# Attention and a patch convolution on one core: scored key tiles and kept score blocks in alternation over the whole chunk

## What is computed

```python
q = einsum('qc,bcn->bqn', Wq, xf); k = einsum('qc,bcn->bqn', Wk, xf)     # 32 rows each
v = einsum('vc,bcn->bvn', Wv, xf)                                        # 256 rows
attn = softmax(einsum('bqn,bqm->bnm', q, k) / sqrt(32), axis=-1)         # 4096 x 4096 per image
out = einsum('bvm,bnm->bvn', v, attn)
y = gamma[0] * einsum('oc,bchw->bohw', Wo, out) + x
# layer 1, per 8x8 patch p of y
low = mean of 2x2 of p;  high = p - up2(low)
low = prelu(bn(mag_w @ low + mag_b));  hs = [high, roll(high, 1, rows)]
out = up2(low) + prelu(bn(phase_w @ hs + phase_b))[:256]
```

## Time and profile before

| | before |
|---|---|
| median of 3 runs | 2342.92 us (2342.83 to 2344.77) |
| the profiled execution | 2340.45 us |
| its span, first to last instruction | 2338.5 us |
| mean granted TensorE clock | 0.984 |
| TensorE busy (matmul) | 2205.9 us, 94% of the span |
| VectorE, ScalarE, GpSimd busy | 76%, 61%, 29% |

### The profile page before, as it was taken

How to read it: one execution, slowest core, us unless ns; L and a number is a source line. 1 busy time by engine, 2 the same in 40 slices (tenths; PEclk the granted TensorE clock), 3 DMA queues, 4 the chain that set the end, 5 groups by cost and what they waited for, 6 DMA issues and landing times.

```text
span 2338.5 us, 48099 instructions
## 1 busy us (share of the span) xinstructions
PE 2205.9 (94%) x16373; PEld 1764.1 (75%) x16373; DVE 1782.4 (76%) x3388; ACT 1431.6 (61%) x2547; POOL 677.7 (29%) x891
## 2 busy tenths in 40 slices
PE   5799999999989999999998999999999999999997
PEld 4577777777767777777777777777777777777776
DVE  6777877777867788877786877777877777778764
ACT  3457666657656666666656666566665656666663
POOL 3232332232322323322232321323322232233321
PEclk8799999999999999999999999999999999999998
DMA  4254444454554444444474443443445444344443
GB/s 159 59 115 94 99 109 102 84 117 99 135 131 85 110 107 92 109 108 97 93 168 102 99 99 72 104 96 91 103 111 133 75 89 93 77 82 88 84 86 64
DMA packets 596617, 235.02 MB, mean 101 GB/s; under 512 B 547072, under 2 KB 548352, under 8 KB 596576
## 3 DMA queue, kind: packets, MB, share of 16 engines
q1 hardware_dynamic: 596576, 234.51, 45.5%
HBM read 67.67 MB, written 32.53 MB: 43 GB/s over the span
## 4 chain that ended last, share of the span: by engine, by line
PE 64%; DVE 15%; issue 10%; DMA 5%; ACT 3%; POOL 1%; SPq 1%; DVEq 0%; ACTq 0%; POOLq 0%
PE M L482 13%; PE M L519 7%; PE O L631 7%; PE O L633 6%; PE O L632 6%; PE O L644 6%; PE O L646 6%; PE O L645 6%; DVE pq L1052 5%; DMA pt<-pq 4%; PE S L590 4%; DVE saved L947 4%; DVE pmax L943 2%; DVE pl L1047 2%; PE M L500 1%
## 5 line engine op out<-in xcount | busy, mean ns | idle before, releaser
L758 ACT ACTIVATE ph<-S 128x512 f16<-128x512 f32 x512 | 307.6, 601 | 525.5 <-PE S L590 524.8
L644 PE MATMUL O<-uh,pt 128*128 128x257 f16 x2048 | 568.2, 277 | 16.9 <-DMA pt<-pq 16.7
L631 PE MATMUL O<-uh,ph 128*128 128x257 f16 x2048 | 570.3, 278 | 4.5 <-DVE pl L1047 4.1
L633 PE MATMUL O<-uh,pl 128*128 128x257 f16 x2048 | 563.2, 275 | 0.0
L632 PE MATMUL O<-ul,ph 128*128 128x256 f16 x2048 | 561.8, 274 | 0.0
L646 PE MATMUL O<-uh,pt 128*128 128x257 f16 x2048 | 559.0, 273 | 0.0
L645 PE MATMUL O<-ul,pt 128*128 128x256 f16 x2048 | 555.7, 271 | 0.0
L947 DVE TENSOR_SCALAR_CACHE_REDUCE saved<-M 128x512 f32<-128x512 f32 x512 | 344.0, 687 | 257.0 <-PE M L519 253.0
L1047 DVE TENSOR_TENSOR pl<-p,ph 128x512 f16<-128x512 f32 x512 | 402.6, 787 | 60.5 <-ACT p L761 59.1
L519 PE MATMUL M<-kst,qst 96*128 (+1 forms) x1024 | 424.0, 442 | 20.9 <-DVE saved L947 16.2
L1052 DVE TENSOR_TENSOR pq<-saved,pq 128x512 f16<-128x512 f32 x512 | 387.6, 757 | 19.2 <-ACT saved L770 19.1
(11 more groups left out here) (161 smaller groups left out, 2907.4 us busy)
## 6 DMA issues: line engine op xcount, KB each, us to landing
xr<-in_x SPq DMA_DIRECT2D x53, 512.0 KB, 3.8
out_y<-z SPq DMA_DIRECT2D x33, 512.0 KB, 3.0
xb<-in_x SPq DMA_DIRECT2D x25, 512.0 KB, 3.7
pt<-pq SPq DMA_TRANSPOSE x512, 3.1
qraw<-q_scratch SPq DMA_DIRECT2D x99, 64.0 KB, 2.0
uh_scratch<-uh_next SPq DMA_DIRECT2D x24, 257.0 KB, 3.2
uh<-uh_scratch SPq DMA_DIRECT2D x24, 257.0 KB, 3.2
ul_scratch<-ul_next SPq DMA_DIRECT2D x24, 256.0 KB, 3.1
```

The lines of the kernel that those rows point to most:

```text
L631: nc.tensor.matmul(O[j][:, 0:UW], ph[:, i % 4, q], uh[:, i, :], start=(i == 0), stop=False)
L633: ins = nc.tensor.matmul(O[j][:, 0:UW], pl[:, i % 4, q], uh[:, i, :], start=False, stop=False)
L644: nc.tensor.matmul(O[j][:, 0:UW], pt[:, k % RING, i, :], uh[:, t, :], start=False, stop=False)
```

## The change

It has three parts.

1. `UNITS` alternates from the first step: d0, k0, d1, k1, to d15, k15. Block k is weighed in step 2k + 1; its exponentials are in step 2k - 4 and its low part in step 2k - 2 (the last one a step earlier). For blocks 0 and 1, and for the low part of block 0, that is before the chunk's first step: they are made at the very start of the chunk.
2. The values in SBUF are waited for by groups of four tiles, each with a semaphore, instead of one for each half; the loads at the end of an image move to the places where their group has been used. O0 to O2 are complete with d15, so they are copied out after it (`d_weighed`), O3 after k15.
3. ScalarE waits for the next image's scale ahead of the first eviction of values, not ahead of the chunk. VectorE starts the reduction before the image (`bound_x`) and makes the scale after step 0's normalising; its first chunk of an image is written out apart from the loop for that.

In the diff, the first `copy_out` and the first `turn` are ScalarE's, the last `turn` is VectorE's.

```diff
-RISE = 6
-UNITS = [("d", i) for i in range(RISE)]
...
+UNITS = [unit for i in range(ND) for unit in (("d", i), ("k", i))]
+EXP_AT = [2 * k - 4 for k in range(NK)]
+LOW_AT = [min(2 * k - 2, MT - 5) for k in range(NK)]
...
             def weigh_tile(g, i):
-                if i == 0:
-                    pe.wait_ge(u_direct_loaded, 128 * (g // NCH) + 16)
+                if i % SUB == 0:
+                    pe.wait_ge(u_loaded[i // SUB], 32 * (g // NCH) + 16)
...
             def weigh_slot(g, k):
-                if k == 0:
-                    pe.wait_ge(u_turned_loaded, 128 * (g // NCH) + 16)
+                if k % SUB == 0:
+                    pe.wait_ge(u_loaded[TURNED[k // SUB]], 32 * (g // NCH) + 16)
...
             def copy_out(g, j):
 
-                act.wait_ge(k_weighed, NK * g + RING - SUB + j + 1)
+                act.wait_ge(d_weighed, ND * g + ND)
...
                 elif kind == "u":
+                    if task[1] == 0:
+                        act.wait_ge(scaled, g // NCH + 2)
                     act.wait_ge(u_stored, 32 * g + 32)
...
             def turn(g, parity, c, plan, scans):
 
+                for k in range(NK):
+                    if EXP_AT[k] < 0:
+                        slot_probabilities(g, k)
                 if plan is FULL:
                     copy_out(g, 0)
                 probabilities(g, 0)
...
-            def before_image(image, parity):
-                act.wait_ge(scaled, image + 2)
...
-            def turn(g, parity, c, plan, scans):
+            def turn(g, parity, c, plan, scans, scale_of=None):
+                for k in range(NK):
+                    if LOW_AT[k] < 0:
+                        slot_low_probabilities(g, k)
...
+                    if t == 0 and scale_of is not None:
+                        find_scale(scale_of + 1, 1 - parity)
```

More of the change, by code:

```diff
@@ L149, in attention_conv @@
         half = sb("half", [128, 2, CT])
-        spare = sb("spare", [128, 10])
+        spare = sb("spare", [128, 10 + NCH])
         quarter = sb("quarter", [128, 1])
@@ L231, in attention_conv @@
         u_stored = sem("u_stored")
-        u_direct_loaded, u_turned_loaded = sem("u_direct_loaded"), sem("u_turned_loaded")
+        u_loaded = [sem(f"u_loaded{m}") for m in range(NCH)]
         o02_out, o13_out, rs_step, on_ready = sem("o02_out"), sem("o13_out"), sem("rs_step"), sem("on_ready")
@@ L270, in turns @@
                 before_image(B - 2, 0)
-            with eng.Fori(0, inner) as c:
+            if image_start:
+                image_start(B - 2, (B - 2) * NCH, 0, scans=False)
+            with eng.Fori(begin, inner) as c:
                 turn((B - 2) * NCH + c, 0, c, FULL, scans=False)
@@ L468, in _ @@
             sp.wait_ge(u_stored, 32 * (1 + ALL - NCH))
-            sp.wait_ge(u_direct_loaded, 16 + 128 * (B - 1))
-            sp.wait_ge(u_turned_loaded, 16 + 128 * (B - 1))
+            for m in range(NCH):
+                sp.wait_ge(u_loaded[m], 16 + 32 * (B - 1))
             sp.wait_ge(xr_loaded, 16 * (1 + ALL))
@@ L874, in _ @@
             nc.vector.memset(spare[:, 2:3], 0.0).then_inc(proj_free, 4)
+            nc.vector.memset(spare[:, 0:1], 0.0).then_inc(d_weighed, ND)
             nc.vector.memset(spare[:, 3:4], 0.0).then_inc(k_weighed, RING)
@@ L877, in _ @@
                 nc.vector.memset(spare[:, 6 + i:7 + i], 0.0).then_inc(turned[i], 16)
-            nc.vector.memset(spare[:, 5:6], 0.0).then_inc(u_direct_loaded, 16)
-            nc.vector.memset(spare[:, 4:5], 0.0).then_inc(u_turned_loaded, 16)
+            for m in range(NCH):
+                nc.vector.memset(spare[:, 10 + m:11 + m], 0.0).then_inc(u_loaded[m], 16)
             dve.wait_ge(consts, 1)
@@ L1028, in copy_out @@
             def copy_out(g, j):
-                dve.wait_ge(k_weighed, NK * g + RING - SUB + j + 1)
+                if j < SUB - 1:
+                    dve.wait_ge(d_weighed, ND * g + ND)
+                else:
+                    dve.wait_ge(k_weighed, NK * g + RING)
                 nc.vector.tensor_copy(oraw[:, j, :], O[j][:, 0:UW]).then_inc(o13_out, 1)
@@ L1136, in before_image @@
                 dve.wait_ge(xs_scanned, image * NCH + 1)
-                find_scale(image + 1, 1 - parity)
-            turns(dve, turn, before_image)
+                bound_x(1 - parity)
+            turns(dve, turn, before_image,
+                  image_start=lambda image, g, parity, scans: turn(g, parity, 0, FULL, scans, scale_of=image))
             copy_out(ALL, 1)
```

61 lines of the change are left out of this document (30 added, 31 removed).

## The result

The changed kernel takes 2587.65 us (median, 2586.90 to 2587.92); the kernel before takes 2342.88 us beside it. The ratio is 1.1044, with a 95% interval of 1.1025 to 1.1063: slower by 245 us, against a forecast of 2568 (2476 to 2640).

A forecast was written before the change was run, and what follows sets the result against it. TensorE, busy in 94% of the span, was taken to bound the kernel, so new waits add in full. Ordinary chunks +183, image starts +1.5 and last image +43 made +227 on 2340.45 us: 2568 us, range 2476 to 2640.

The forecast's parts named there:

- Block 0: Ordinary chunk's start: transpose 0, queued behind the queries' store, lands at T + 8.85; TensorE waits 4.0 us.
- Blocks 1 and 2: Ordinary chunk: no wait for block 1; block 2, behind the stores, leaves the chunk 7.4 us late, block 0's 4.0 included.
- Block 4: Ordinary chunk: a deadline possibly missed behind the load of half a megabyte, within the rest's chance of 0.04.
- The chunk's end: Maxima's transpose waits 0.45 us more, and tile 15's low part comes 0.8 late: together 1.3 us.
- The sum of an ordinary chunk: 7.4 for blocks, 1.3 chunk's end, less 0.5 for today's block 2 wait, plus 0.5 clock: 8.7 us.
- The clock: Lower granted clock behind TensorE's waits: 0.5 us in an ordinary chunk as a mean, 1.2 in the last image's chunks.
- the clock falls in every chunk: Rival: up to 2.7 us of clock loss in each of 31 chunks, +63 us, 2631 us; chance 0.20.
- The image start: Chunks 0, 8, 16: today's extra 7.5, 9.8 and 7.3 us go, each start gains 8.7: +1.5 us in all.
- The last image: Seven chunks: 4.4 us wait before block 1, 0.45 at the maxima's transpose, 1.2 clock: 6.1 us each, 43 in all.
- A transpose's time: Issue to landing of a block's transpose: trace median 3.1 us used, not the skill page's estimate of 2.6.
- Only block 0 counts: Rival: block 2's wait disappears, an ordinary chunk costs 5.3 us, +146 us, 2486 us; chance 0.22.
- Faster: Rival: transposes 0 to 2 early enough, transpose 0 issued by T + 1.7, only image starts change: 2316 us; chance 0.04.

The follow-up runs named there:

- t0_first: Changed kernel with transpose 0 ahead of the load of xb and the store of the queries in SyncE's queue: 2537.85 us, 1.0833.
- exp2_later: Changed kernel with block 2's two exponentials one step later on ScalarE, behind the copy of keys and queries: 2567.73 us, 1.0956.
- t012_first: Changed kernel with transposes 0, 1 and 2 ahead of the queries' store and fetch and the stores of values and output: 2399.15 us, 1.0241.
- early_but_pl15: Changed kernel with transposes 0, 1, 2 and 4 earlier in SyncE's queue, block 2's exponentials a step later, its low part a step earlier: 2351.32 us, 1.0039.
- scale_ahead: Changed kernel with VectorE and ScalarE waiting for the scale ahead of the image, as before the change: 2624.64 us, 1.1213.
- t01_first: Changed kernel with transpose 0 ahead of the queries' store and transpose 1 ahead of the queries' fetch: 2477.03 us, 1.0585.
- pl15_first: Changed kernel with VectorE's low part of direct tile 15 made ahead of the bias, not behind it: 2606.24 us, 1.1137.

## Why the prediction was right, step by step

**What bounds the kernel.** The premise held: TensorE had 6% of slack, and each new wait was added in full. 187 of the 247 us are idle time of TensorE, 52 its clock and 8 other busy time.

**Block 0.** The forecast had qraw out at T + 5.17, the transpose at T + 5.75, the landing at T + 8.85 and a wait of 4.0 us. Measured from T = 410.30: 5.14, 5.90, 9.01 and 3.94. t0_first shows that the queue makes the wait, exp2_later that block 2's exponentials are 1.2 us of it.

**Blocks 1 and 2.** No wait for block 1 was forecast, with 0.3 us to spare, and none came. Block 2 was to land at T + 20.5; it landed at T + 21.7, and the wait was 2.5 us, inside "2 to 3.5" (1.9 to 2.8 in the ordinary chunks). The 1.2 us are not a wrong order but nearly all the slow clock behind block 0: score 3 was out at T + 11.8 and not at T + 10.7. One slip did no harm by luck: the terms written down for the store of the values add up to T + 14.3, not to T + 14.6, and the way from ScalarE's eviction to that store took 0.95 us (424.99 to 425.94) where 0.7 was taken. t012_first shows that the stores ahead of transpose 2 are the cause.

**Block 4** was named as a milder possibility and not counted. It costs 0.5 to 1.0 us in 19 of the 21 ordinary chunks and hardly anything in two, 0.7 as a mean.

**The chunk's end** was put at 1.3 us. Tile 15's wait is 0.56 (forecast 0.8), but the 0.45 at the maxima's transpose did not come: that wait fell from 0.35 to 0.29 us. The pauses of TensorE in front of it are not the reason, since it is 0.28 us in early_but_pl15 too, where they are gone; the count of VectorE's work at the chunk's end was too high, and by what is open. In the last image, with one wait, it grew from 1.67 to 1.90, half of what was said.

**The sum of an ordinary chunk.** Of the 8.7 us forecast, 8.2 were waits and 0.5 clock; of the 9.55 measured, 7.2 are idle and 2.3 busy time. The waits by steps, against the forecast and as means of the ordinary chunks: blocks 0 and 2 together 1.2 less (7.4 late in all, measured 3.9 + 2.3; the slow clock fills a part of that time with work), block 4 0.7 more, the chunk's end 0.8 less, small ones 0.3 more. Busy time is 1.8 more than the 0.5. Together 0.8. The chunk takes 79.2 us where 78 to 79 was to show it, and TensorE's share is 87.6%, just over the 87% named. That the total came within 20 us of the measured time is in part luck: waits counted 1.0 us too high and a clock counted 1.6 too low in each ordinary chunk cancel for the greater part.

**The clock** is the term that was mis-sized most. The forecast had 0.5 us for an ordinary chunk and 1.2 in the last image; TensorE's busy time grew by 49.1 / 21 = 2.3 and 12.8 / 7 = 1.8, of which the granted clock makes 2.1 and 1.8. What speaks for a small term there is a wrong reading: the prediction says that the longest wait for a block in the kernel before, 2.7 us, lies in a stretch granted full speed. Before it the clock was full; behind it, it was 0.60 and 0.55 for 4 us.

```profile
127.14 0.28 PE L644 MATMUL O<-uh,pt 128*128 128x257 f16 x1 [2.67 <-DMA pt<-pq]
```

```profile
128.00:130.00 2.00, 2.00 (x10) 1.32 (x9) 0.37 (x1) 0.80 (x2) 0.79 (x2) 0.60 0.67 245
```

The rival "the clock falls in every chunk", which had 0.20 against the forecast's 0.50, had the right mechanism. Its price of up to 2.7 us is not far off, though the losses that it was read from were 2.9 and 1.5 us by the granted clock, not 3.7 and 2.7. The time did not reach its 2631 mainly since the waits stayed 1.0 us a chunk below the sum. The Trainium skill, page "TensorE: Matmul & The Clock Gate", section "HAM oscillation — how this bites in real kernels", describes a TensorE that comes back cold each round after waiting for a DMA; by that rule, the trace agrees: 0.98 or 0.96 as the mean of every ordinary chunk, and 1.00 again in t012_first, whose ordinary chunks have no wait for a block over 0.94 us.

**The image start.** The forecast was three chunks like the ordinary ones. Their mean is 79.28 us, that of an ordinary chunk 79.17. scale_ahead shows the 11 us a start that this part takes away, more than the 9.8, 7.3 and 7.5 of the sum: at the start of image 1 its 8.1 us for the scale come on top of the waits for blocks, which are 8.3 us there with it and without it, and the rest is clock.

**The last image**: forecast 6.1 us a chunk, measured 6.4; the wait before block 1 was put at 4.4 and is 4.26 in six of the seven chunks. t01_first shows that the fetch ahead of transpose 1 makes it.

**A transpose's time.** The Trainium skill, page "DMA: Bandwidth & Descriptors", section "Anatomy of one DMA", gives a fixed cost and a rate, and from them comes the estimate of 2.6 us for one, by which the sum would have been some 30 us smaller. The changed kernel's block 0 took 3.1 us from issue to landing (416.20 to 419.31), so the trace's own number was the one to use.

**The rivals.** "Only block 0 counts" (2486) fell with the 2.5 us before block 2. "Faster" needed transpose 0 at T + 1.7; it came at T + 5.9. And with the transposes early the new order is still not faster (2351), although the gain of the scale part is in that time.

## What to carry to other kernels

When units are weighed in another order, the queue that feeds them has to be put into that order too: for each one, write down what stands ahead of its transfer in the queue and what that waits for, and count from there. A wait taken away at one transfer shows up at the next one in the queue until all of them are moved, so undo them one by one, in the order of the queue. And a change in parts should be measured in parts: here the one about the scale gained 13 to 15 us by itself, 22 when it was taken further, hidden in a loss of 245.

## What was not expected of the hardware

The granted clock fell to 0.50 behind a wait of 2.75 us in exp2_later and stayed at 1.00 behind one of 2.83 us in t01_first and one of 3.71 us in the changed kernel. The same low-part instruction of VectorE took 1.17 us at one place (pl15_first) and 0.68 at others. The traces show what goes with it: it took 0.9 to 1.2 us wherever one of GpSimd's two-operand instructions was under way when it started (110 of 512 in the kernel before, 120 in the changed kernel), and 0.7 us wherever none was (402 and 392; in 31 of the latter one had less than 0.1 us to go). No run moved GpSimd's work to try it. GpSimd's reduction across partitions spent 5.5 to 8.0 us, in all traces, between the instruction before it and the start of its own row, while that row takes 0.4 to 0.6 us: it has to be started that much ahead.
